# The gathered rows of a group read back by two DMAs on two queues in place of one, in the weighted sums of a graph network

## What is computed

```python
x_l = (x @ Wl + bl).reshape(n, H, C)
...
m = jax.nn.leaky_relu(x_l[src_f] + x_r[dst_f] + e, NEG_SLOPE)
alpha = jnp.einsum('ehc,hc->eh', m, att)
...
aexp = jnp.exp(alpha - amax[dst_f])
asum = jax.ops.segment_sum(aexp, dst_f, num_segments=n)
alpha = aexp / (asum[dst_f] + 1e-16)
out = jax.ops.segment_sum(x_l[src_f] * alpha[..., None], dst_f, num_segments=n)
```

## Time and profile before

| | us |
|---|---|
| median of 3 runs | 5740.17 |
| lowest, highest | 5734.01, 5756.72 |
| the profiled execution's own time | 5702.34 |
| its span, first to last instruction | 5700.5 |
| weighted sums, from 3757.5 to 4065.0 of the span | 307.5 |

### The profile page before, as it was taken

One profiled execution on the slowest core, in us unless ns is written; L12 is line 12 of the kernel. 1 busy time (PEld: TensorE's weight loads), 2 busy tenths in 40 slices (PEclk: granted clock), 3 DMA queues, 4 the chain that ended last, 5 costly groups with the idle time before them and its releaser, 6 DMA issues.

```text
span 5700.5 us, 61044 instructions
## 1 busy us (share of the span) xinstructions
PE 3324.1 (58%) x19159; PEld 3100.7 (54%) x19160; DVE 2808.7 (49%) x3801; ACT 1675.3 (29%) x2774; POOL 2048.7 (36%) x1982
## 2 busy tenths in 40 slices
PE   1300000019999999544444444357479999689697
PEld 0300000019999999544333343246379789589597
DVE  8300000024454544677666677788954344544345
ACT  0000000005645455200000000023266356456265
POOL 2777666750000000377677777346300000200300
PEclk9999999999999999755555555579789999799798
DMA  9700000008858587499899899247368268478585
GB/s 356 275 1 16 1 1 1 1 12 278 257 183 276 175 275 227 126 228 220 215 216 214 215 221 222 62 122 214 92 205 277 84 208 277 151 244 285 180 283 183
DMA packets 887483, 1008.44 MB, mean 177 GB/s; under 512 B 391651, under 2 KB 651705, under 8 KB 887270
## 3 DMA queue, kind: packets, MB, share of 16 engines
q1 hardware_dynamic: 795778, 861.50, 51.6%
q0 software_dynamic: 56208, 63.97, 4.8%
q10 hardware_dynamic: 35284, 80.30, 3.6%
HBM read 692.09 MB, written 233.14 MB: 162 GB/s over the span
## 4 chain that ended last, share of the span: by engine, by line
PE 44%; another core or an unknown queue 23%; DVE 14%; issue 11%; POOL 3%; ACT 2%; DMA 2%; DVEq 1%; SPq 0%; ACTq 0%; POOLq 0%
PE banks L918 35%; PE banks L841 4%; POOL work L624 2%; PE banks L1000 2%; DVE Z L1397 1%; DVE big L1519 1%; DVE Z L1402 1%; PE banks L863 1%; ACT banks L779 1%; DVE big L1406 1%; DMA work<-tab,stage 1%; DVE Z L1404 1%; ACT X L668 1%; PE banks L966 1%
## 5 line engine op out<-in xcount | busy, mean ns | idle before, releaser
L918 PE MATMUL banks<-wides,rows 128*128 128x384 f32 (+2 forms) x11040 | 2028.5, 344 | 155.8 <-issue 88.6
L918 PEld LDWEIGHTS banks<-wides,rows 128*128 128x128 f32 x11040 | 1949.4, 189 | 229.1 <-issue 94.3
L624 POOL DMA_INDIRECT work<-tab,stage x832 | 902.8, 1085 | 1483.0 <-ACT stage L771 1232.2
L1265 DVE CAST wides<-big 128x768 fp32r<-128x768 f16 (+3 forms) x1429 | 811.1, 569 | 1176.7 <-PE banks L918 1072.3
L698 ACT CAST wides<-big 128x768 fp32r<-128x768 f16 (+2 forms) x1037 | 832.2, 804 | 677.9 <-PE banks L918 554.3
L598 POOL DMA_INDIRECT cells<-queue_i x784 | 787.0, 1004 | 311.9 <-issue 298.6
L972 PE MATMUL banks<-V,work 128*128 x1664 | 372.5, 414 | 378.6 <-ACT work L773 312.1
L972 PEld LDWEIGHTS banks<-V,work 128*128 128x128 f32 x1664 | 345.1, 316 | 415.9 <-issue 415.9
L650 POOL DMA_INDIRECT V<-tab,nodei x100 | 96.2, 962 | 1201.9 <-DMA tab<-X 879.8
L863 PE MATMUL banks<-work 128*128 128x50 f16 x784 | 92.1, 278 | 670.6 <-issue 600.5
L863 PEld LDWEIGHTS banks<-work 128*128 128x128 f16 x784 | 73.1, 149 | 689.5 <-issue 612.6
(11 more groups left out here) (300 smaller groups left out, 3229.1 us busy)
## 6 DMA issues: line engine op xcount, KB each, us to landing
big<-cells SPq DMA_DIRECT2D x490, 416.0 KB
big<-cells SPq DMA_DIRECT2D x441, 384.0 KB
big<-turned SPq DMA_DIRECT2D x300, 384.0 KB
gathered<-work SPq DMA_DIRECT2D x104, 512.0 KB
work<-gathered SPq DMA_DIRECT2D x104, 512.0 KB, 4.2
big<-turned SPq DMA_DIRECT2D x100, 416.0 KB
cells<-work ACTq DMA_DIRECT2D x98, 416.0 KB, 14.6
turned<-big SPq DMA_DIRECT2D x50, 800.0 KB
```

What stands on the lines that cost most here:

```text
L624: pool.indirect_dma_start(msg[:, j, u, :], None, tab[0][:, :], bass.IndirectOffsetOnAxis(ap=stage[:, j * U + u:j * U + u + 1].bitcast(U32) ...
L918: last = pe.matmul(banks[:, 4 * (w % 2) + j, 0:(z - a) * P], rows2[:, s, part * D:(part + 1) * D], wides[:, q % QUEUE, (a - start) * P:(z ...
L1265: dve.tensor_copy(wides[:, (2 * m + 1) % QUEUE, 0:(z - a) * P], halves[:, m % HALVES, a * P:z * P]).then_inc(s_wided, 1)
```

## The change

The 512 KB read of a group is cut into two of 256 KB, each 4 of the 8 visits. SP still reads the first half, under the same wait. The second half is issued on ACT's queue: in ACT's loop over the groups, ahead of the wait for and the clear of the group's PSUM slot, ACT now waits for `s_mm` with the same value as SP and issues the DMA. It signals a semaphore of its own (`s_back_b`), and POOL waits for both.

```diff
@@
         s_back = [sem(f"s_back{j}") for j in range(RING)]
+        s_back_b = [sem(f"s_back_b{j}") for j in range(RING)]
@@
                         sp.wait_ge(s_mm, i * RING + (GROUPS + j + 1))
-                        sp.dma_start(msg[:, j, :, :], gathered[bass.ds(i * (RING * P) + j * P, P), :].rearrange("p (u f) -> p u f", u=U)).then_inc(s_back[j], 16)
+                        sp.dma_start(msg[:, j, 0:U // 2, :], gathered[bass.ds(i * (RING * P) + j * P, P), 0:U * D // 2].rearrange("p (u f) -> p u f", f=D)).then_inc(s_back[j], 16)
@@
                     pool.wait_ge(s_back[j], i * 16 + 16)
+                    pool.wait_ge(s_back_b[j], i * 16 + 16)
@@
             with act.Fori(0, ROUNDS) as i:
                 for j in range(RING):
+                    act.wait_ge(s_mm, i * RING + (GROUPS + j + 1))
+                    act.dma_start(msg[:, j, U // 2:U, :], gathered[bass.ds(i * (RING * P) + j * P, P), U * D // 2:U * D].rearrange("p (u f) -> p u f", f=D)).then_inc(s_back_b[j], 16)
                     act.wait_ge(s_sum, i * RING + (j + 1))
                     act.copy(gslots[j % 2], zeros[:, 0:1].rearrange("p (a b) -> p a b", b=1).to_broadcast([P, 3, 3 * GW])).then_inc(s_clear, 1)
```

## The result

The changed kernel is slower: ratio 1.0129 to the kernel before, 95% interval 1.0102 to 1.0156. The median of four runs is 5818.6 us against 5737.8. The two medians are 81 us apart, and the ratio of 1.29% makes 74 us of 5738; 54 were forecast, and 5794 had been given with a range of 5757 to 5840.

The account below looks back on a forecast made before the run. DVE's pace of 2.67 us a group was taken to bound the weighted sums, with no one bound for the whole kernel; 101 groups x 0.54 us gave +54 us, 5740 + 54 = 5794, range 5757 to 5840.

Parts of the forecast that it names:

- What bounds the stage: Weighted sums: DVE nearly full, 2.67 us a group; rows lie ready 2.0 us, so a faster read buys nothing.
- SP's half and POOL's second wait: Read-back of rows: SP's 256 KB lands ahead of need and POOL's extra semaphore test fits in 0.15 us; each worth 0.
- ACT's half, a loop of three groups: ACT's DMA stands behind the previous group's clear, closing a loop of 9.62 us, 3.21 a group, 0.54 more than 2.67.
- The sum, +54 us: Weighted sums: 101 of 104 groups each 0.54 us longer; start between 0 and +2 us, middle taken as 0.
- the clock: PE in the weighted sums: pauses lower its clock, matmuls take 4.03 us, loop 3.84 a group, +118 us, 5858; chance 0.06.
- the main case: Weighted sums: ACT's half lands in 2.7 to 4.1 us, 3.04 to 3.51 us a group, +37 to +85 us; chance 0.64.
- the stretch at 66% in the earlier trace: Another stretch, PE busy 66% at granted clock 0.91; cited against a clock fall at the forecast 67% in the weighted sums.
- The range, 5757 to 5840: Whole kernel, us: from a small read landing fast to ACT's DMA waiting for the clear's end; excludes clock, no change, faster.
- The rival of a DMA that waits for the clear to end: ACT's queue: DMA goes only after the clear ends, loop 1.2 us longer, 3.61 a group, +95 us, 5835; chance 0.13.
- The small read, 2.05 us: ACT's half: landing goes wholly with size, loop 8.47 us, 2.82 a group, +15 us, 5755; chance 0.09.
- Nothing changes: ACT's queue: its half goes out when SP's does, so the time stays 5740; chance 0.05.
- Signs named: Weighted sums: adds 3.2 us apart, about a hundred PE waits for POOL, stage about 360 us; clock below 0.9 means wrong.

Follow-up runs that it names:

- the two profiles: The changed kernel profiled twice, the second time unaltered on another chip: ratios 1.0129 and 1.0134 to the kernel before, adds spanning 371.3 and 356.9 us.

## Why the prediction was right

- **What bounds the stage.** Right. DVE's pace with rows that lie ready for 2 us; both halves on SP, 1.0010, show that a smaller or sooner read buys nothing.
- **SP's half and POOL's second wait, 0.** Right, shown by the same run.
- **ACT's half, a loop of three groups.** Right, and shown by moving the DMA one group either way. Its terms, in the turn above: 0.22 us to the DMA (0.2 forecast), landing 2.74 (3.2; the median of all groups is 3.0), the rest 6.46 (6.22). Together 9.42 (9.62), which is one of the shortest turns. The better test is the run with more matmuls, 3.208 a group at full clock (3.21).
- **The sum, +54 us.** The loop's part came out: at full clock it is 50 us by the two profiles and 55 by the run with more matmuls. What was mis-sized is the clock, put at nothing in the main case and at 64 us on top of it (118 in all) in a rival with a chance of 0.06. It was neither: 22 to 26 us in one execution and 7 to 12 in another, which bring the loop's part to the 77 and 62 us of the adds; the ratio gives 74 us. The forecast spoke of a pause of a microsecond in each group. The trace shows about 1 us or less ahead of two groups and then some 2 us or more, so the stretch at 66% in the earlier trace rows was no guide to which groups begin at the lower level.
- **The range, 5757 to 5840.** It held with 5818.6, but it left the clock out, and its upper part stood for a late landing and a late issue, neither of which came. That the clock's share fitted into it was luck.
- **The rival of a DMA that waits for the clear to end.** Fell: it went out 0.22 us after the clear's start, 0.46 in every fourth group.
- **The small read, 2.05 us.** Fell with 3.0 us. The 2.7 us of the 448 KB store was no guide: a read of the same size landed in 3.7.
- **Nothing changes, for which the Trainium skill's sentence stood.** Fell. The Trainium skill (DMA: Bandwidth & Descriptors, Issuing engines are not separate DMA queues) states that issuing from several engines saves only the sequencer's time. The run with ACT's half one group earlier agrees with it: a second engine, and ratio 0.9994. With the half behind the clear of the group before it is 1.0129; what the issuing engine has to wait for first, the sentence does not cover. The run with both halves on SP (1.0010) has one issuing engine and does not test it.
- **Signs named.** Adds 3.2 us apart: 3.49 for the groups 10 to 48, with the clock. PE waiting for POOL about a hundred times: 47 times with 102.1 us in all, since within a burst some groups are released by ACT (28 times). The stage about 360 us long: 384.6. The forecast also named a sign of being wrong that did come: the granted clock of the stage fell below 0.9, to 0.88. It marks the term that was mis-sized, and not the loop, which the runs with the DMA moved show. ACT's issue at 0.2 us, its landing at 3.2 and its lag behind SP's half came as named.

## What to carry to other kernels

In this kernel the DMA on ACT's queue was released by what stood ahead of it in ACT's order, not by its own wait alone. Write down which instruction it stands behind and what that one waits for, count how many groups the closed loop spans, and compare its length divided by that number with the pace; if it is longer, issue the DMA one group earlier, which here took 1.3% to nothing. And before a transfer is split or moved, look whether anyone waits for it: here, apart from the start, it was waited for in one gap, and that gap had another cause.

## What the runs showed of the hardware

- ACT's DMA went out 0.22 us (0.46 in every fourth group) after the start of a 1.19 us copy ahead of it, so its queue does not wait for the copy to end. From group 3 on it did not go out before that copy had started, though SP's DMA under the same wait had gone 4.9 us earlier (median): the queue does hold it while the copy ahead waits for its semaphore.
- Reads into 512-byte pieces landed 2.2, 3.0, 3.7 and 4.2 us (medians) after their issue for 64, 256, 448 and 512 KB.
- More work can cost less. With pauses of PE after each burst of three groups, the 16 matmuls of 30 of the 104 groups took 2.4 to 4.0 us in place of 2.14, at a granted clock of 0.88 for the stage; with 25% more matmuls the steady part was at 1.00 and the stage 22 us shorter.
